# Three more VectorE instructions behind a softmax's reciprocal, and a row maximum kept in bf16

## The chip, the cores and the metric

The program runs on the 8 cores of one Trainium2 chip. Each core works on its own 4096 rows of the activations, and no data passes between cores. The time is that of the slowest core, in microseconds of the device.

## What is computed

One transformer layer: attention over the heads of each token, then a gated feed-forward part, each behind a layer normalisation and with a residual.

```python
def _L0_attn_ref(x, Wq, Wk, Wv, Wfc):
    h, hd = (16, 64)
    Q = (x @ Wq.T).reshape(b, s, h, hd)
    K = (x @ Wk.T).reshape(b, s, h, hd)
    V = (x @ Wv.T).reshape(b, s, h, hd)
    scores = jnp.einsum('bshd,bstd->bsht', Q, K) / math.sqrt(hd)
    attn = jax.nn.softmax(scores, axis=-1)
    out = jnp.einsum('bsht,bstd->bshd', attn, V).reshape(b, s, dm)
    return out @ Wfc.T
x = x + _L0_attn_ref(_layernorm(x, axis=-1), ...)       # x: (4, 8192, 1024)
x = x + _L0_ffn_ref(_layernorm(x, axis=-1), ...)        # 1024 -> 3072 -> 1024, SiLU gate
```

The attention is between the 16 heads of one token: for each of a core's 4096 tokens there is a 16x16 matrix of scores, and its softmax weighs the 16 value vectors of that token. There is no product over the sequence.

## The kernel before

The program has three stages with a barrier between them.

1. Weights (L214 to L307): all weights are transposed by TensorE. The four attention matrices stay in SBUF, the three of the feed-forward part go to HBM.
2. Attention (from L311): 32 tiles of 128 tokens, a token a partition. This stage holds the change.
3. Feed-forward: 8 blocks of 512 tokens, with weights streamed from HBM.

A small scheduler (`Sched`) keeps one list of instructions for each engine. `S.add(engine, fn, waits=..., chain=..., inc=...)` appends to it, so the order of the Python calls is the order on each engine. `chain=True` makes an instruction wait for the one before it on the same engine, by a semaphore; `waits` names other engines' semaphores.

In the attention stage a tile k goes through these steps:

- `load_tile`, `ln1_a`, `ln1_b`, `lnt`, `proj`: the tile `xcT` is loaded, ScalarE takes the sums for the normalisation (L348, L354), VectorE (DVE) makes mean and variance in single columns of `Lr` with two `tensor_scalar`, a product (L369) and a difference (L371), ScalarE takes logarithm and exponential (L374, L378), DVE writes the normalised tile (`xnm`, L382), TensorE transposes it and makes Q, K and V, and ScalarE copies these to `Qs`, `Ks`, `Vs` (L463).
- `front(k)`: the scores, on DVE. For each of four groups g of four heads: the product `gramB` of Q and K (L475, 4096 columns), the add of its two halves (`gh`, L487, 2048 columns) and a sum to 64 scores in `Ss` (L499). Then the maximum over the 16 scores of each head (`Sm`, L508), the subtraction (L516), and the exponential on ScalarE (L523), which leaves `Se`.
- `back_a(k)`: the sum of the exponentials (`Sl`, L532), its reciprocal (`Sr`, L537) and the weights `Aa` (L543) on DVE; then four products `avB` of weights and values on GpSimd (POOL), one for each group (L552). `avB` has two buffers, so groups 2 and 3 wait until TensorE has read groups 0 and 1.
- `back_a2(k)`: TensorE sums `avB` with the identity into `pOT` (L577), ScalarE copies it to `OT` (L593).
- `back_b(k)`: the output projection (L611), and the residual on DVE (`x1p`, L623), whose statistics ScalarE takes.
- `back_b2(k)`: the second normalisation with the same lines L363 to L382 (`xn2m`), eight transposes (L657) and their copies.

The steps of different tiles are interleaved by hand. The slot of tile k is, in the order of the calls: `front(k)`, `back_a(k - 1)`, `back_a2(k - 2)`, `back_b(k - 3)`, `back_b2(k - 4)`, and then, in three of four slots, the normalisation and projections of a tile of the next block (one tile in two of them, two tiles in the third). Behind the last slot follow `back_a(31)` and the rest of the open steps.

The lines that the change touches or surrounds:

```python
323  Sm = e(nc.sbuf_tensor("Sm", [128, 16], F32))
326  Sr = e(nc.sbuf_tensor("Sr", [128, 16], F32))
537  S.add("vector", lambda e: e.reciprocal(Sr[:], Sl[:]), chain=True)
```

Of the kernel before, what the change touches and what calls it, by code (L numbers as in the profile page):

```python
# [7 lines left out]
F32 = mybir.dt.float32  # L8
BF16 = mybir.dt.bfloat16
I32 = mybir.dt.int32  # L10
AF = mybir.ActivationFunctionType
ALU = mybir.AluOpType
# [78 lines left out]
def build_program(taps=(), stop_after=None):  # L91
# [5 lines left out]
    nc = bass.Bass("TRN2", target_bir_lowering=False)  # L97
# [37 lines left out]
    with ExitStack() as TOP:  # L135
# [91 lines left out]
        with ExitStack() as ph:  # L227
            e = ph.enter_context
# [5 lines left out]
            S = Sched(cnt, hwm)  # L234
# [76 lines left out]
        with ExitStack() as ph:  # L311
            e = ph.enter_context
# [7 lines left out]
            Ks = [e(nc.sbuf_tensor(f"Ks{t}", [128, 1024], BF16)) for t in range(4)]  # L320
            Vs = [e(nc.sbuf_tensor(f"Vs{t}", [128, 1024], BF16)) for t in range(8)]
            Ss = e(nc.sbuf_tensor("Ss", [128, 256], F32))
            Sm = e(nc.sbuf_tensor("Sm", [128, 16], F32))
            Se = [e(nc.sbuf_tensor(f"Se{i}", [128, 256], BF16)) for i in range(4)]
            Sl = e(nc.sbuf_tensor("Sl", [128, 16], F32))
            Sr = e(nc.sbuf_tensor("Sr", [128, 16], F32))
            Aa = [e(nc.sbuf_tensor(f"Aa{i}", [128, 256], BF16)) for i in range(4)]
            gramB = [e(nc.sbuf_tensor(f"gramB{i}", [128, 4096], BF16))
                     for i in range(2)]
# [11 lines left out]
            S = Sched(cnt, hwm)  # L341
# [185 lines left out]
            def back_a(k):  # L527
                s, tt = divmod(k, 4)
                e4 = k % 4
                S.add("vector",  # L530
                      lambda e, e4=e4:
                      e.reduce_sum(Sl[:, 0:16].rearrange("p (a b) -> p a b", b=1),  # L532
                                   bass.AP(Se[e4][:].tensor, Se[e4][:].offset,
                                           [[256, 128], [1, 16], [16, 16]]),
                                   AX.X),
                      waits=[("aex", k + 1)])
                S.add("vector", lambda e: e.reciprocal(Sr[:], Sl[:]), chain=True)  # L537
                am_w = []
                if ("pool", k - 4) in cap:
                    am_w.append(("apl", cap["pool", k - 4]))  # L540
                S.add("vector",
                      lambda e, e4=e4:
                      e.tensor_tensor(Aa[e4][:].rearrange("p (t h) -> p t h", h=16),  # L543
                                      Se[e4][:].rearrange("p (t h) -> p t h", h=16),
                                      bass.AP(Sr[:].tensor, Sr[:].offset,
                                              [[16, 128], [0, 16], [1, 16]]),
                                      ALU.mult),
                      waits=am_w, chain=True, inc="amx")
                for g in range(4):
                    S.add("gpsimd",  # L550
                          lambda e, e4=e4, g=g, k=k:
                          e.tensor_tensor(  # L552
                              avB[g % 2][:].rearrange("p (t h d) -> p t h d",
                                                      t=4, d=64),
                              bass.AP(Aa[e4][:].tensor, Aa[e4][:].offset + 64 * g,
                                      [[256, 128], [16, 4], [1, 16], [0, 64]]),
                              bass.AP(Vs[k % 8][:].tensor,
                                      Vs[k % 8][:].offset + 256 * g,
                                      [[1024, 128], [64, 4], [0, 16], [1, 64]]),
                              ALU.mult),  # L560
                          waits=[("amx", k + 1), ("aot", 4 * k + g - 1)],
                          inc="apl")
                cap["pool", k] = S.n("apl")
# [125 lines left out]
            def a1(k):  # L689
                if k >= 0:  # L690
                    back_a(k)
# [83 lines left out]
        with ExitStack() as ph:  # L775
# [17 lines left out]
            S = Sched(cnt, hwm)  # L793
# [129 lines left out]
```

How the kernel before makes its waits and increments, by code:

```python
                    def f(e):  # L71
                        for op in ops:
                            waits = list(op["waits"])
                            for tok in op["deps"]:
                                waits.append(selfcount[tok])
                            for (s, v) in waits:
                                key = (eng_name, s)
                                if v > 0 and hwm.get(key, 0) < v:
                                    e.wait_ge(sems[s], v)
                                    hwm[key] = v
                            ins = op["fn"](e)
                            if op["inc"] is not None:
                                ins.then_inc(sems[op["inc"]], op["incn"])
                            elif op["selfneed"]:
                                ins.then_inc(sems["sf" + eng_name], 1)
# [71 lines left out]
                    def f(e, k=k):  # L157
                        e.nop().then_inc(sems["ph"], 1)
                        e.wait_ge(sems["ph"], NENG * k)
# [7 lines left out]
                @blk.sync  # L167
                def _(sy):
                    t0 = cnt.get("tapd", 0)
                    add = [0]
                    def issue(dst, src):
                        sy.dma_start(dst, src).then_inc(sems["tapd"], 16)
                        add[0] += 16
                    for (_, fn) in todo:
                        fn(issue)
                    sy.wait_ge(sems["tapd"], t0 + add[0])
                    cnt["tapd"] = t0 + add[0]
```

## Time and profile before

| | us |
|---|---|
| three runs | 3925.12, 3932.15, 3969.2 |
| median | 3932.15 |
| the profiled execution | 3932.16 |
| its slowest core's span | 3930.3 |
| spans of all cores | 3898.4 to 3930.3 |

Busy time on the slowest core, in us: TensorE's matmuls 2275.6 (58% of the span), DVE 2040.3 (52%), POOL 1131.8 (29%), ScalarE 685.1 (17%). These shares are averages over three stages with different limits. In the page's 40 slices of the span DVE is at 6 to 9 tenths from slice 7 to slice 26, which is the attention stage, and at 1 tenth behind it, where TensorE goes to 7 to 9. The page says that busy spans on POOL are rough, and that an engine's idle time costs nothing where the engine doesn't set the pace.

### The profile page before, as it was taken

The page shows a single profiled execution, that of the slowest core. Times are in us where ns is not written, and L with a number is a line of the kernel's source. Part 1 is how long each engine was busy: PE and PEld are TensorE (multiplying, and loading weights), DVE is VectorE, ACT ScalarE, POOL GpSimd, SP SyncE. Part 2 cuts the span into 40 slices and gives each one's busy share as a digit, 9 for nine tenths or more (in the row PEclk, how much of TensorE's full clock was granted, in tenths as well). Part 3 has the DMA queues.
Part 4 walks back from the last instruction along what each step waited for, and adds up shares of the span by engine and source line. Part 5 has one row for each costly group of instructions (what it writes and reads, how often), then busy time and mean ns, then how long its engine had stood idle before and what let it go on. Part 6 is the DMA issues. An engine that isn't in the chain of part 4 may idle for free. (4 is left out here: it accounts for less than half of the span.)

```text
span 3930.3 us, 38110 instructions; the slowest of 8 cores (3898.4 to 3930.3 us)
## 1 busy us (share of the span) xinstructions
PE 2275.6 (58%) x12352; PEld 1179.2 (30%) x12352; DVE 2040.3 (52%) x2209; ACT 685.1 (17%) x1691; POOL 1131.8 (29%) x450
## 2 busy tenths in 40 slices
PE   4333354544545345453554453468869788797887
PEld 2111122232323233222232232323324333343333
DVE  5433369786977887869868789411111111111111
ACT  0122231212122212121221211121101111010110
POOL 1000005444444464536344545601101011010110
PEclk9999986766667666667665676689989999999999
DMA  5446300001000001000000000034445444443443
GB/s 94 126 153 203 114 19 1 22 11 33 11 22 22 22 17 27 22 22 22 11 23 21 27 6 11 22 113 140 150 138 159 130 149 142 151 159 126 153 144 140
DMA packets 109629, 302.38 MB, mean 77 GB/s; under 512 B 13184, under 2 KB 29568, under 8 KB 108416
## 3 DMA queue, kind: packets, MB, share of 16 engines
q1 hardware_dynamic: 68736, 159.41, 13.1%
q0 software_dynamic: 32640, 121.65, 10.1%
q10 hardware_dynamic: 8064, 18.88, 1.2%
q8 instruction: 108, 1.77, 0.2%
q14 instruction: 81, 0.66, 0.1%
HBM read 247.46 MB, written 60.82 MB: 78 GB/s over the span
## 5 line engine op out<-in xcount | busy, mean ns | idle before, releaser
L552 POOL TENSOR_TENSOR avB<-Aa,Vs 128x4096 bf16<-128x4096 bf16 x128 | 964.6, 7556 | 1237.9 <-PE pOT L577 761.4
L577 PE MATMUL pOT<-ident,avB 128*128 128x128 bf16 x4096 | 370.4, 275 | 349.5 <-POOL avB L552 349.5
L839 DVE TENSOR_TENSOR hseg<-sg,pU 128x512 bf16<-128x512 bf16 x192 | 132.0, 688 | 710.9 <-PE pU L834 683.7
L577 PEld LDWEIGHTS pOT<-ident,avB 128*128 128x128 bf16 x4096 | 353.0, 127 | 368.2 <-issue 363.2
L820 PE MATMUL pG<-x2s,wgS 128*128 128x512 bf16 x1536 | 376.0, 389 | 125.2 <-DMA wgS<-d_wgT 124.1
L475 DVE TENSOR_TENSOR gramB<-Qs,Ks 128x4096 bf16<-128x4096 bf16 x128 | 420.7, 3286 | 29.0 <-ACT Vs L463 15.4
L834 PE MATMUL pU<-x2s,wuS 128*128 128x512 bf16 x1536 | 370.0, 384 | 19.7 <-DMA wuS<-d_wuT 19.6
L487 DVE TENSOR_TENSOR gh<-gramB 128x2048 bf16<-128x2048 bf16 x128 | 356.0, 2781 | 14.0 <-DVE gramB L475 0.9
L862 PE MATMUL pD<-hseg,wdC 128*128 128x512 bf16 x1536 | 350.2, 385 | 15.9 <-DMA wdC<-d_wdT 14.6
L274 PE MATMUL wps<-ident,wstg_b 128*128 128x128 bf16 x832 | 190.4, 264 | 286.0 <-ACT wstg_b L253 133.4
L657 PE MATMUL pT<-ident,xn2m 128*128 128x128 bf16 x256 | 54.4, 268 | 514.0 <-DVE xn2m L382 479.8
L809 POOL DMA_DIRECT2D wuS<-d_wuT x192 | 103.1, 537 | 805.9 <-PE pU L834 752.8
L499 DVE TENSOR_REDUCE Ss<-gh 128x64 f32<-128x2048 bf16 x128 | 292.6, 2286 | 13.6 <-DVE gh L487 0.5
L879 DVE TENSOR_TENSOR yst<-pT,x1s 128x128 f32<-128x128 f32 x256 | 64.0, 287 | 434.5 <-PE pT L872 434.2
L296 DVE CAST wpk<-wps 128x128 bf16<-128x128 f32 x576 | 142.9, 287 | 209.4 <-PE wps L274 207.8
L820 PEld LDWEIGHTS pG<-x2s,wgS 128*128 128x128 bf16 x1536 | 149.7, 99 | 320.9 <-issue 156.4
L825 ACT ACTIVATE sg<-pG 128x512 bf16<-128x512 f32 x192 | 114.6, 597 | 678.8 <-PE pG L820 678.7
L834 PEld LDWEIGHTS pU<-x2s,wuS 128*128 128x128 bf16 x1536 | 151.4, 99 | 210.9 <-issue 38.1
L862 PEld LDWEIGHTS pD<-hseg,wdC 128*128 128x128 bf16 x1536 | 147.8, 99 | 195.6 <-issue 32.1
L274 PEld LDWEIGHTS wps<-ident,wstg_b 128*128 128x128 bf16 x832 | 86.6, 104 | 389.7 <-issue 362.1
L371 DVE TENSOR_TENSOR Lr<-Lr 128x1 f32<-128x1 f32 x64 | 191.2, 2988 | 7.2 <-DVE Lr L369 0.8
L657 PEld LDWEIGHTS pT<-ident,xn2m 128*128 128x128 bf16 x256 | 25.3, 104 | 553.4 <-issue 547.0
(78 smaller groups left out, 2032.6 us busy)
## 6 DMA issues: line engine op xcount, KB each, us to landing
wuS<-d_wuT POOLq DMA_DIRECT2D x192, 256.0 KB, 3.3
wgS<-d_wgT SPq DMA_DIRECT2D x192, 256.0 KB, 2.6
wdC<-d_wdT POOLq DMA_DIRECT2D x64, 768.0 KB, 4.5
xcT<-x SPq DMA_DIRECT2D x32, 512.0 KB, 5.7
d_x<-x1p SPq DMA_DIRECT2D x32, 512.0 KB, 3.8
x1s<-d_x SPq DMA_DIRECT2D x8, 2048.0 KB, 14.8
y<-yst SPq DMA_DIRECT2D x32, 512.0 KB, 4.3
wstg_i<-wg SPq DMA_DIRECT2D x24, 512.0 KB, 3.9
```

The source lines that it names most:

```text
L274: e.matmul(wps[b % 2][:, 0:128], wstg_b[j % 4][:, b * 128:(b + 1) * 128], ident[:], start=True, stop=True),
L296: e.tensor_copy(pdst(e), wps[b % 2][:, 0:128]),
L371: Sch.add("vector", lambda e: e.tensor_sub(Lrt[:, 5:6], Lrt[:, 3:4], Lrt[:, 4:5]), chain=True, inc="aln")
L475: e.tensor_tensor(gramB[g % 2][:].rearrange("p (t h d) -> p t h d", t=4, d=64), bass.AP(Qs[tt][:].tensor, Qs[tt][:].offset, [[1024, 128], ...
L487: e.tensor_tensor(gh1[:].rearrange("p (a b) -> p a b", b=32), bass.AP(gramB[g % 2][:].tensor, gramB[g % 2][:].offset, [[4096, 128], [64, 6 ...
L499: e.tensor_reduce(Ss[:, 64 * g:64 * (g + 1)] .rearrange("p (a b) -> p a b", b=1), gh1[:].rearrange("p (a b) -> p a b", b=32), AX.X, ALU.add),
L552: e.tensor_tensor(avB[g % 2][:].rearrange("p (t h d) -> p t h d", t=4, d=64), bass.AP(Aa[e4][:].tensor, Aa[e4][:].offset + 64 * g, [[256, ...
L577: e.matmul(pOT[:, 128 * b:128 * (b + 1)], avB[g % 2][:, 1024 * i + 128 * b: 1024 * i + 128 * (b + 1)], ident[:], start=(g == 0 and i == 0 ...
L820: e.matmul(pG[h % 2][:], wgS[h % 2][:, j * 128:(j + 1) * 128], x2buf[xp][j][:], start=(j == 0), stop=(j == 7)),
L834: e.matmul(pU[h % 2][:], wuS[h % 2][:, j * 128:(j + 1) * 128], x2buf[xp][j][:], start=(j == 0), stop=(j == 7)),
L839: lambda e, h=h: e.tensor_mul(hseg[h][:], sg[h % 2][:], pU[h % 2][:]),
L862: e.matmul(pD[c % 2][:], wdC[c % 2][:, k * 128:(k + 1) * 128], hseg[k][:], start=(k == 0), stop=(k == 23)),
```

## The change

The maximum `Sm` is kept in bf16 where it was f32. Behind the reciprocal three instructions are added on DVE, each on 128x16 f32 and each waiting for the one before: `Snr = Sl * Sr`, `Snr = 2 - Snr`, `Sr = Sr * Snr` (one Newton step on the reciprocal). `Aa` follows as before.

```diff
-            Sm = e(nc.sbuf_tensor("Sm", [128, 16], F32))
+            Sm = e(nc.sbuf_tensor("Sm", [128, 16], BF16))
             Se = [e(nc.sbuf_tensor(f"Se{i}", [128, 256], BF16)) for i in range(4)]
             Sl = e(nc.sbuf_tensor("Sl", [128, 16], F32))
             Sr = e(nc.sbuf_tensor("Sr", [128, 16], F32))
+            Snr = e(nc.sbuf_tensor("Snr", [128, 16], F32))
@@
                 S.add("vector", lambda e: e.reciprocal(Sr[:], Sl[:]), chain=True)
+                S.add("vector", lambda e: e.tensor_mul(Snr[:], Sl[:], Sr[:]),
+                      chain=True)
+                S.add("vector",
+                      lambda e: e.tensor_scalar(Snr[:], Snr[:], -1.0, 2.0,
+                                                ALU.mult, ALU.add),
+                      chain=True)
+                S.add("vector", lambda e: e.tensor_mul(Sr[:], Sr[:], Snr[:]),
+                      chain=True)
```

## Rows read from the trace of the kernel before

**Rows 1.** Busy us and instruction count of each engine in the attention stage.

```profile
core 5: us, PE busy (x) PEld busy (x) DVE busy (x) ACT busy (x) POOL busy (x), PEclk, DMA share, GB/s
485.00:2590.00 2105.00, 997.66 (x6656) 619.33 (x6656) 1630.74 (x928) 457.64 (x1377) 964.56 (x128) 0.68 0.07 20
```

**Rows 2.** POOL's waits in that stage: us in total, times, longest.

```profile
POOL avB L552 <- PE pOT L577: 761.4, 32, 45.0
POOL avB L552 <- DVE Aa L543: 476.5, 31, 237.0
```

**Rows 3.** Single lines of DVE: duration ns min/median/max, first and last start.

```profile
L475 DVE TENSOR_TENSOR gramB<-Qs,Ks x128: 2291/2293/8669, 531.3 to 2467.9; 128x4096 bf16<-128x4096 bf16 x128
...
L487 DVE TENSOR_TENSOR gh<-gramB x128: 1224/1226/7867, 533.7 to 2470.3; 128x2048 bf16<-128x2048 bf16 x128
...
L371 DVE TENSOR_TENSOR Lr<-Lr x64: 158/160/6883, 490.2 to 2579.7; 128x1 f32<-128x1 f32 x64
...
L516 DVE TENSOR_TENSOR Se<-Ss,Sm x32: 425/426/3994, 556.4 to 2474.7; 128x256 bf16<-128x256 f32 x32
...
L543 DVE TENSOR_TENSOR Aa<-Se,Sr x32: 425/426/427, 583.5 to 2493.4; 128x256 bf16<-128x256 bf16 x32
...
L363 DVE TENSOR_SCALAR Lr<-Lr,c_ni x64: 213/214/216, 489.3 to 2578.8; 128x1 f32<-128x1 f32 x64
```

**Rows 4.** Time line of DVE, 2470 to 2494: start us, us, instruction, idle before it.

```profile
2475.77 0.25 DVE L537 RECIPROCAL Sr<-Sl 128x16 f32<-128x16 f32 x1
2476.12 0.42 DVE L543 TENSOR_TENSOR Aa<-Se,Sr 128x256 bf16<-128x256 bf16 x1
2476.47 0.68 DVE L623 TENSOR_TENSOR x1p<-pA,xcT 128x512 f32<-128x512 f32 x1
...
2478.49 5.30 DVE L369 TENSOR_TENSOR Lr<-Lr 128x1 f32<-128x1 f32 x1
2483.90 6.88 DVE L371 TENSOR_TENSOR Lr<-Lr 128x1 f32<-128x1 f32 x1
2491.57 0.81 DVE L382 TENSOR_SCALAR xn2m<-x1p,Lr 128x1024 bf16<-128x1024 f32 x1 [0.79 <-ACT Lr L378]
...
2493.36 0.42 DVE L543 TENSOR_TENSOR Aa<-Se,Sr 128x256 bf16<-128x256 bf16 x1
```

**Rows 5.** Time lines of POOL and then of DVE, 2154 to 2229, two places of the second pair.

```profile
2154.44 15.11 POOL L552 TENSOR_TENSOR avB<-Aa,Vs 128x4096 bf16<-128x4096 bf16 x2 [29.17 <-PE pOT L577]
2171.45 14.02 POOL L552 TENSOR_TENSOR avB<-Aa,Vs 128x4096 bf16<-128x4096 bf16 x2 [1.90 <-DVE Aa L543]
2211.62 16.06 POOL L552 TENSOR_TENSOR avB<-Aa,Vs 128x4096 bf16<-128x4096 bf16 x2 [26.16 <-PE pOT L577]
...
2154.80 7.86 DVE L487 TENSOR_TENSOR gh<-gramB 128x2048 bf16<-128x2048 bf16 x1
...
2165.84 3.99 DVE L516 TENSOR_TENSOR Se<-Ss,Sm 128x256 bf16<-128x256 f32 x1
...
2212.75 8.05 DVE L475 TENSOR_TENSOR gramB<-Qs,Ks 128x4096 bf16<-128x4096 bf16 x1
2220.90 7.86 DVE L487 TENSOR_TENSOR gh<-gramB 128x2048 bf16<-128x2048 bf16 x1
```

**Rows 6.** Groups of DVE by line, same shape: busy us, mean ns, idle before, releaser.

```profile
L290 DVE TENSOR_SCALAR WqJ<-wps,c_qk 128x128 bf16<-128x128 f32 x64 | 19.5, 347 | 20.8 <-PE wps L274 20.8
...
L296 DVE CAST WvJ<-wps 128x128 bf16<-128x128 f32 x64 | 15.7, 287 | 11.0 <-PE wps L274 11.0
```

**Rows 7.** Time line of POOL behind the last slot.

```profile
2499.18 27.98 POOL L552 TENSOR_TENSOR avB<-Aa,Vs 128x4096 bf16<-128x4096 bf16 x4 [8.42 <-PE pOT L577]
```

**Rows 8.** Groups of DVE by line: busy us, mean ns, idle before, releaser.

```profile
L371 DVE TENSOR_TENSOR Lr<-Lr 128x1 f32<-128x1 f32 x64 | 191.2, 2988 | 7.2 <-DVE Lr L369 0.8
L516 DVE TENSOR_TENSOR Se<-Ss,Sm 128x256 bf16<-128x256 f32 x32 | 35.0, 1094 | 3.3
```

## The prediction

> **What bounds the kernel now.** I read the page first: the chain that ended last lies almost wholly in the feed-forward stage, so it says nothing about the stage that is edited. The next view is therefore busy time by stage [rows 1]. Attention takes 2105.00 us, with VectorE (DVE) busy for 1630.74 us (77%) at a granted TensorE clock of 0.68; the feed-forward stage is TensorE's and has none of the edited lines. Everything that the edit can do, it does in these 2105 us, that is 65.8 us for each of 32 tiles.
>
> Then who waits for whom [rows 2]. GpSimd (POOL) waits in two places: for `Aa` (L543), 31 times, 476.5 us in all, and for TensorE's `pOT` matmuls, 32 times. So POOL works through a tile's four `avB` products in two pairs: groups 0 and 1 start as soon as DVE has written `Aa`, groups 2 and 3 when TensorE has read group 0. With one exception, which comes below, POOL is idle when `Aa` is being made.
>
> Then how long single instructions take [rows 3]. A `gramB` product takes 2.29 us at its median and up to 8.67, the add `gh` 1.23 and up to 7.87, and a subtraction on one column of `Lr` (L371) 0.16 and up to 6.88. The surplus is 6.4 to 6.7 us at most, and in the time lines [rows 4, 5] it falls where POOL runs an `avB` product, itself 7.0 us (a pair is 14.01): a DVE instruction with two operands in SBUF stands still while POOL holds its product, and the other way round. `Aa`, with the same kind of operands, never does: 425 to 427 ns in all 32.
>
> The time line of DVE around one `Aa` [rows 4] shows what sets the pace. `Aa` starts at 2476.12. POOL begins right behind it. DVE goes on with `x1p` and the statistics, meets the lock at L369 (5.30 us instead of 0.16), meets it again at L371 (6.88), and is through at 2490.78, 14.66 us after the start of `Aa`, which is POOL's pair plus a start of 0.6. ScalarE's two steps, `xn2m` (2491.57), the transposes on TensorE and the `pOT` matmuls follow, and these release POOL's second pair. Hence everything in a tile hangs from the start of `Aa`; a wait of `x1p` for TensorE ahead of L369 is swallowed by the same lock.
>
> **The change part by part.** (a) Three DVE instructions on 128x16 f32 are put between the reciprocal (L537) and `Aa` (L543), each waiting on the one before. The cost is a duration and the gap that a chained successor shows.
>
> Duration of a multiplication: L371 does one column in 0.160 us at its median [rows 3] and L543 does 256 in 0.426, so a column costs (0.426 - 0.160)/255 = 1.04 ns, and 16 columns 0.160 + 15 x 0.00104 = 0.176 us. Duration of the two-operation `tensor_scalar` with written-out numbers: there is no such row. L363, with its factor read from memory, takes 0.214 for one column [rows 3], so 0.230 for 16: the upper bound. Reading a factor costs about 0.347 - 0.287 = 0.060 at equal shape (L290 against the plain copy L296 [rows 6]); less that, 0.170. I take 0.175, nearer to the plain form, because the new one has no factor in memory either; both ends stay for the range.
>
> Gap: L537 starts at 2475.77, lasts 0.25, and `Aa` starts at 2476.12, 0.10 after its end [rows 4]; L369 ends at 2483.79 and L371 starts at 2483.90, 0.11 behind. I take 0.105. Without a wait the next one starts earlier: `x1p` starts at 2476.47, 0.07 before the end of `Aa`. The Trainium skill (VectorE: DVE Perf Modes, The DRAIN you can't avoid) says that a semaphore behind each VectorE instruction costs nothing over one behind the last. By that rule alone the sum would be the three durations, 0.53 us a tile or 16 us; the trace here disagrees with it, since chained and unchained neighbours differ by some 0.18 us in their starts.
>
> Per tile: 3 x 0.105 + 2 x 0.176 + 0.175 = 0.84 us. The upper end with the slower `tensor_scalar` is 0.90. If the gaps didn't count it would be 0.53.
>
> How many tiles are exposed? Each tile whose `Aa` POOL waits for, 31 [rows 2]. The last one isn't: its `Aa` starts at 2493.36, while POOL starts at 2499.18 on four products in a row, the first two of them the second pair of the tile before, because TensorE held it up [rows 7]. That tile's first own product begins some 20 us after its `Aa`, and this covers 0.84 us easily. If that cover were gone, it would cost 0.84 us. Sum: 31 x 0.84 = 26.0 us; the upper end 31 x 0.90 = 27.9.
>
> Nothing cushions it on the other queues. Behind the chained instructions stand `Aa`, `x1p` and the statistics on DVE; POOL waits for `Aa`, ScalarE for the statistics, TensorE for `xn2m` and for POOL. All start later by the same amount, so the distances between POOL's second pair and DVE's `gramB`, `gh` and reduction stay as they are, because all of these come after `Aa`.
>
> (b) `Sm` becomes bf16. The reduction that writes it (L508) still reads 256 f32 columns, the subtraction (L516) still reads `Ss` in f32. L516 unheld takes 0.426 us, as long as L543 [rows 3], so I put this at nothing. If all of L516's columns went twice as fast, it would save 256 x 1.04/2 = 0.13 us a tile, 4 us; that is the other bound. (c) `Snr` is 64 bytes a partition: no time.
>
> Sum: the profiled execution took 3932.16 us (span 3930.3), the median of the three shown is 3932.15, so both bases agree. 3932 + 26 = 3958 us, up by 0.7%. About 1% (39 us) is what a measurement of this kernel can tell from no change.
>
> **The rivals.**
>
> *A new multiplication meets POOL's lock (slower).* The Trainium skill (SBUF — State Buffer, Who interferes with whom) states the rule: a VectorE instruction with two SBUF inputs and a GpSimd instruction that reads SBUF exclude each other for a whole instruction. In this kernel the mechanism is in the rows: L371 waits up to 6.7 us. Both new multiplications are of this kind. If they met the lock in every tile as L371's group does on average, (191.2/64 - 0.16) = 2.8 us each [rows 8], it would be 31 x 5.6 = 175 us and 4133 us in all. It decides for slower from two meetings of 6.7 us on (26 + 13.4 is over 39). For it: six times L516 has been held by 3.57 us just ahead (3.99 against 0.426; (35.0 - 32 x 0.426)/3.57 = 6.0 [rows 5, 8]). Against it: after such a hold POOL has done its fourth product and idles 1.90 us until `Aa` [rows 5], and it gets no new work before `Aa`, behind the new instructions. The trace bears the rule out, but not its case here.
>
> *The second pair changes its place (slower, or less slow).* Its place among DVE's instructions decides what it costs. At 2154.44 POOL asks while `gramB` runs: `gh` loses 6.63 and L516 3.57, 10.2 us together. At 2211.62 it asks 1.13 us ahead of `gramB`: that loses 5.76 and `gh` 6.63, 12.4 us [rows 5]. In the first case 0.36 us more and POOL would have met `gh` already running; earlier by 2 us, the dear case. TensorE's speed between `xnm` and `pOT` sets it, and its clock is between its levels (1.2 and 2.4 GHz) over the stage, 0.68 on average [rows 1]. If the six cheap tiles turned dear: 6 x 2.2 = 13 us, 3971 us; six dear turned cheap: 3945 us. Against both: all of it hangs from `Aa`, as above.
>
> *The delay is hidden.* If half of the tiles had 0.84 us of slack behind `Aa` (TensorE setting the pace by itself), 13 us would be left: 3945 us. For it: `pOT` is POOL's longer wait, 761.4 us [rows 2]. Against it: that wait starts from `xn2m`, so from `Aa`.
>
> **How the numbers follow.** Forecast as reckoned (3952 to 3965): 0.63. Dear places: 0.17, about 3971, some 0.12 of it over the 1% mark. Lock on the new multiplications: 0.05, over 3971. Hidden or cheap places, or a faster L516: 0.15, 3930 to 3950. Slower by over 1%: 0.12 + 0.05 = 0.17. Faster by over 1% needs 65 us less than reckoned, for which no row has a source: 0.02, out of the last case. Within 1%: 0.81. The range takes the hidden case's 3944 and the dear places' 3974.
>
> **What would show it.** Three new groups of 32 on DVE, near 176, 175 and 176 ns with maxima equal to medians (lock: maxima near 6.9 us). From the start of L537 to that of L543: 1.19 us instead of 0.35. L543's 426 and POOL's 31 waits for `Aa` stay. The stage grows by 26 us and the feed-forward stage by nothing. L516's mean stays at 1.09 us if the second pair keeps its place; a fall means dear tiles. Wrong would be: the stage grown by much less with the three groups in full (slack), gaps near zero (the skill's rule), or a `tensor_scalar` far from 0.18 us.

## The result, and the profile after

Against 15 runs of the kernel before (median 3927.41 us) the changed kernel has a median of 3964.59 us over 15 runs. Some runs of both kernels are slower by up to several per cent, with a lower granted clock on the cores of one die or of both; ratios are taken over the other runs alone. That ratio is 1.0089, with a 95% interval of 1.0066 to 1.0113: 26 to 44 us slower, at the middle 35. All ratios below are against the kernel before, measured on the same chip as the run that they belong to.

In the changed kernel's numbering the lines move by one behind L326 and by nine behind the new instructions: `gramB` is L476, `gh` L488, the subtraction L517, the reciprocal L538, the new ones L539, L542 and L545, `Aa` L552, `avB` L561, the statistics L370 and L372, `xn2m` L383.

Groups of VectorE (DVE) by line, after: busy us, mean ns, idle before (they answer to [rows 3, 8]).

```profile
L476 DVE TENSOR_TENSOR gramB<-Qs,Ks 128x4096 bf16<-128x4096 bf16 x128 | 433.7, 3388 | 29.9 <-ACT Vs L464 16.3 <-DVE Ss L500 0.5
...
L372 DVE TENSOR_TENSOR Lr<-Lr 128x1 f32<-128x1 f32 x64 | 218.6, 3415 | 6.7
...
L517 DVE TENSOR_TENSOR Se<-Ss,Sm 128x256 bf16<-128x256 f32 x32 | 34.6, 1082 | 3.7 <-DVE Sm L509 0.5
...
L552 DVE TENSOR_TENSOR Aa<-Se,Sr 128x256 bf16<-128x256 bf16 x32 | 13.6, 425 | 3.5 <-DVE Sr L545 0.3
...
L539 DVE TENSOR_TENSOR Snr<-Sl,Sr 128x16 f32<-128x16 f32 x32 | 5.6, 176 | 3.7 <-DVE Sr L538 0.5
L545 DVE TENSOR_TENSOR Sr<-Sr,Snr 128x16 f32<-128x16 f32 x32 | 5.6, 175 | 3.7 <-DVE Snr L542 0.5
L542 DVE TENSOR_SCALAR Snr<-Snr 128x16 f32<-128x16 f32 x32 | 5.6, 175 | 3.4
```

The three new groups have the durations that were worked out, and `Aa` is as fast as before. What has grown beside them is `gramB`: its group was busy for 420.7 us before and is for 433.7 now, with the same 128 instructions of the same size. The slowest core, whose rows these are, is core 5 before and core 0 after; on core 0 alone `gramB` went from 418.7 to 433.7 us.

The time line of DVE around one `Aa`, after: start us, us, instruction (it answers to [rows 4]).

```profile
2462.41 0.25 DVE L538 RECIPROCAL Sr<-Sl 128x16 f32<-128x16 f32 x1
2462.76 0.17 DVE L539 TENSOR_TENSOR Snr<-Sl,Sr 128x16 f32<-128x16 f32 x1
2463.05 0.17 DVE L542 TENSOR_SCALAR Snr<-Snr 128x16 f32<-128x16 f32 x1
2463.32 0.17 DVE L545 TENSOR_TENSOR Sr<-Sr,Snr 128x16 f32<-128x16 f32 x1
2463.60 0.42 DVE L552 TENSOR_TENSOR Aa<-Se,Sr 128x256 bf16<-128x256 bf16 x1
...
2465.97 5.30 DVE L370 TENSOR_TENSOR Lr<-Lr 128x1 f32<-128x1 f32 x1
2471.38 6.88 DVE L372 TENSOR_TENSOR Lr<-Lr 128x1 f32<-128x1 f32 x1
2479.05 0.81 DVE L383 TENSOR_SCALAR xn2m<-x1p,Lr 128x1024 bf16<-128x1024 f32 x1 [0.79 <-ACT Lr L379]
```

From the reciprocal to `Aa` it is 1.19 us, as against 0.35 [rows 4], and 1.20 at most in 29 of the 32 tiles. `Aa` to the end of L372 is 14.66 us, `Aa` to `xn2m` 15.45 us, as before. So a tile's work behind `Aa` has moved as a block.

On core 0, from the first `xnm` to the last `xn2m`, attention took 2080.3 us before (498.1 to 2578.4) and takes 2123.0 after (498.1 to 2621.1): 42.7 us more; the eight cores lie between 37.7 and 44.5, 41 in the mean. That is 26 for the new instructions and some 15 beyond them. The extra is not spread evenly. Here are the tiles of the two profiled cores, core 5 before and core 0 after. From one `Aa` to the next, tiles whose second pair keeps its place grow by 0.84 us (14, 29 and 31), some by a third of a us more (in tiles 8, 12, 24 and 30 one pause between two DVE instructions is 0.46 us where it is else 0.11; nothing in the trace says why). Call a place of the second pair dear if POOL asks for it ahead of `gramB`, and cheap if it asks while `gramB` runs. Tiles with one projection have swapped dear and cheap places among themselves (four grow by 3.1 to 3.9 us, four shrink by 1.5 to 2.0), which comes out even at 0.9 us each. But four of the nine tiles whose second pair meets no projection on TensorE grow by 3.3 to 3.4 us. One of them, tile 16, goes from 53.81 to 57.20. Here is its DVE time line, then POOL's.

```profile
1583.37 2.29 DVE L500 TENSOR_REDUCE Ss<-gh 128x64 f32<-128x2048 bf16 x1
1585.76 9.10 DVE L476 TENSOR_TENSOR gramB<-Qs,Ks 128x4096 bf16<-128x4096 bf16 x1
1594.96 7.86 DVE L488 TENSOR_TENSOR gh<-gramB 128x2048 bf16<-128x2048 bf16 x1
...
1585.69 16.06 POOL L561 TENSOR_TENSOR avB<-Aa,Vs 128x4096 bf16<-128x4096 bf16 x2 [7.76 <-PE pOT L586]
```

The same tile in the kernel before, DVE and then POOL:

```profile
1563.71 2.29 DVE L475 TENSOR_TENSOR gramB<-Qs,Ks 128x4096 bf16<-128x4096 bf16 x1
1566.11 7.86 DVE L487 TENSOR_TENSOR gh<-gramB 128x2048 bf16<-128x2048 bf16 x1
...
1576.46 6.54 DVE L475 TENSOR_TENSOR gramB<-Qs,Ks 128x4096 bf16<-128x4096 bf16 x1
...
1564.11 16.75 POOL L552 TENSOR_TENSOR avB<-Aa,Vs 128x4096 bf16<-128x4096 bf16 x2 [8.24 <-PE pOT L577]
```

Before, POOL asked for its second pair 0.40 us after `gramB` had started and waited for it. Now it asks 0.07 us ahead of `gramB`, which then stands for 6.8 us; `gh` behind it loses 6.6 us in either case. Before, the next `gramB` (1576.46) lost another 4.2 us; so the place costs 13.4 instead of 10.9. POOL's second pair is asked for 22.88 us behind `Aa` before and 22.41 behind it after. That is TensorE's doing. Busy us and instructions of TensorE, weight loads, DVE, ScalarE and POOL, then the granted clock, in the stretch in which it begins to read the first pair (18.2 to 23.0 us behind `Aa`), before and after:

```profile
1559.43:1564.23 4.80, 4.47 (x41) 4.11 (x41) 4.49 (x4) 3.10 (x8) 0.12 (x1) 0.50 0.00 0
```

```profile
1581.48:1586.28 4.80, 4.46 (x53) 4.12 (x53) 4.49 (x4) 3.09 (x8) 0.59 (x1) 0.65 0.00 0
```

The granted clock was at its lower level (0.50, 1.2 GHz) over the whole stretch before, and after the change the upper one (2.4 GHz) was granted for the last part of it. TensorE read the pair half a microsecond sooner, and so POOL came in ahead of `gramB`. In the three other tiles that grew so, the same stretch had 0.56 to 0.58 before and has 0.64 to 0.67; in the five that stayed cheap it has 0.50 to 0.56 after.

Half a microsecond is the distance between two cores, though. Core 0 had 0.62 in this stretch of tile 16 before the change, and asked 22.51 us behind `Aa`. `gramB` starts 22.48 behind it, so the place was cheap by 0.03 us, and 0.10 us less (22.41) made it dear. All eight cores show the same edge. In the 72 tiles without a projection (nine on each core), every request up to 22.47 us behind `Aa` meets a dear place (56.4 us or more before, 57.1 or more after) and every later one a cheap place (54.1 at most before, 55.3 after). Three of the 72 were dear before, 29 are after.

### The profile page after: what moved, and what is told of

Same layout as the page of the kernel before. It is cut to its first block and busy times, and to the rows that moved or that the text cites. A ratio compares the mean times of both kernels' runs of the same rounds, so it can differ in the third digit from the quotient of the medians.

```text
span 3968.3 us, 38302 instructions; the slowest of 8 cores (3936.1 to 3968.3 us)
## 1 busy us (share of the span) xinstructions
PE 2262.6 (57%) x12352; PEld 1172.7 (30%) x12352; DVE 2086.0 (53%) x2305; ACT 685.4 (17%) x1691; POOL 1134.6 (29%) x450
## 5 line engine op out<-in xcount | busy, mean ns | idle before, releaser
L561 POOL TENSOR_TENSOR avB<-Aa,Vs 128x4096 bf16<-128x4096 bf16 x128 | 967.0, 7576 | 1278.2 <-PE pOT L586 758.3
L476 DVE TENSOR_TENSOR gramB<-Qs,Ks 128x4096 bf16<-128x4096 bf16 x128 | 433.7, 3388 | 29.9 <-ACT Vs L464 16.3
L488 DVE TENSOR_TENSOR gh<-gramB 128x2048 bf16<-128x2048 bf16 x128 | 356.0, 2781 | 14.0 <-DVE gramB L476 0.9
L372 DVE TENSOR_TENSOR Lr<-Lr 128x1 f32<-128x1 f32 x64 | 218.6, 3415 | 6.7
```

The costliest lines, as they stand in the source:

```text
L372: Sch.add("vector", lambda e: e.tensor_sub(Lrt[:, 5:6], Lrt[:, 3:4], Lrt[:, 4:5]), chain=True, inc="aln")
L476: e.tensor_tensor(gramB[g % 2][:].rearrange("p (t h d) -> p t h d", t=4, d=64), bass.AP(Qs[tt][:].tensor, Qs[tt][:].offset, [[1024, 128], ...
L488: e.tensor_tensor(gh1[:].rearrange("p (a b) -> p a b", b=32), bass.AP(gramB[g % 2][:].tensor, gramB[g % 2][:].offset, [[4096, 128], [64, 6 ...
L561: e.tensor_tensor(avB[g % 2][:].rearrange("p (t h d) -> p t h d", t=4, d=64), bass.AP(Aa[e4][:].tensor, Aa[e4][:].offset + 64 * g, [[256, ...
```

## The experiments

**Theory A**: a tile's pace hangs from the start of `Aa`. A chain ahead of it costs its length in 31 tiles; the rest of the loss is where POOL's second pair falls. **Theory B**: the bf16 `Sm` makes the part that the sum lacks. **Theory C**: DVE is the bound, and each microsecond of its work costs one wherever it stands.

**1. The three instructions alone.** `Sm`, which nobody needs any more at this point, takes the place of `Snr`, so that no array is added.

```diff
-Sm = ... BF16
+Sm = ... F32
-e.tensor_mul(Snr[:], Sl[:], Sr[:]) ...
+e.tensor_mul(Sm[:], Sl[:], Sr[:]) ...      # and so in the other two
```

> The three instructions alone; `Sm` stays f32 and also takes the place of `Snr`, since SBUF is full. Theory A (the chain ahead of `Aa` costs 0.84 us in each of 31 tiles, and the rest of the 37 us comes from POOL's second pair falling ahead of `gramB` in some tiles): 26 us plus 0 to 15 us for the places, so 1.007 to 1.010 of before; spacing of the four starts 0.28 us. Theory B (bf16 of `Sm` makes the 11 us that the sum lacks): exactly the 26 us, 1.0066.

Measured: ratio 1.0102, interval 1.0079 to 1.0125. The three groups are at 175 ns, and `gramB` is at 432.6 us, nearly as in the changed kernel.

The cores of this run also differ in TensorE's clock. Over the attention stage cores 4 and 5 were granted 0.668, cores 0 to 3 0.693 to 0.695. On the two slower-clocked cores `gramB` was busy for 387.0 and 380.8 us, and none of their nine tiles without projections was dear; on the other four it was 430.9 to 433.2 us, with three or four dear tiles each. The stage took 2099 and 2097 us on the two, and 2119 to 2122 on the four: with the lower clock it was shorter.

**2. The bf16 maximum alone.**

```diff
-Sm = e(nc.sbuf_tensor("Sm", [128, 16], F32))
+Sm = e(nc.sbuf_tensor("Sm", [128, 16], BF16))
```

> `Sm` in bf16 alone. Theory A: nothing, 0.998 to 1.002, with L508 at 0.58 us and L516 at 0.43 us unheld. Theory B: about 11 us, 1.003. If the subtraction went faster in bf16: 0.30 us instead of 0.43 and up to 4 us less.

Measured: ratio 0.9987, interval 0.9975 to 0.9998; L516 has the mean of before (1094 ns), L508 as well (580), `gramB` 420.8 us. Its middle is 5 us under the kernel before, and no row of the trace has that as a gain. Theory B falls with these two runs: the whole loss comes with the three instructions, none of it with bf16.

**3. The same three behind `Aa`.** They write to `Sm`, which nobody reads, so the Newton step has no effect on the output here.

```diff
                       waits=am_w, chain=True, inc="amx")
+                S.add("vector", lambda e: e.tensor_mul(Sm[:], Sl[:], Sr[:]), chain=True)
+                S.add("vector", lambda e: e.tensor_scalar(Sm[:], Sm[:], -1.0, 2.0, ALU.mult, ALU.add), chain=True)
+                S.add("vector", lambda e: e.tensor_mul(Sm[:], Sr[:], Sm[:]), chain=True)
```

> The same three instructions, chained, on the same operands, but behind `Aa` and with their result going to a tile that nobody reads, so the Newton step itself has no effect. Theory A (a tile's pace hangs from the start of `Aa`, and what stands between `Aa` and L371 is swallowed by POOL's first pair): -5 to +8 us, ratio 0.999 to 1.002, with L371 still ending 14.7 us after the start of `Aa`, and the third new instruction waiting up to 7 us for POOL. Theory C (VectorE is the bound and each microsecond of its work costs one): 26 to 37 us, 1.007 to 1.009.

Measured: ratio 1.0299, interval 1.0268 to 1.0330, some 117 us slower. Neither theory had this. The time line of DVE:

```profile
1508.60 0.43 DVE L543 TENSOR_TENSOR Aa<-Se,Sr 128x256 bf16<-128x256 bf16 x1
1509.14 0.17 DVE L549 TENSOR_TENSOR Sm<-Sl,Sr 128x16 f32<-128x16 f32 x1
1509.42 6.88 DVE L552 TENSOR_SCALAR Sm<-Sm 128x16 f32<-128x16 f32 x1
1516.40 6.88 DVE L555 TENSOR_TENSOR Sm<-Sr,Sm 128x16 f32<-128x16 f32 x1
1523.20 0.68 DVE L631 TENSOR_TENSOR x1p<-pA,xcT 128x512 f32<-128x512 f32 x1
...
1527.60 0.81 DVE L382 TENSOR_SCALAR xn2m<-x1p,Lr 128x1024 bf16<-128x1024 f32 x1 [1.96 <-ACT Lr L378]
```

The first multiplication slips in before POOL starts, the other two wait out one product of the pair each. The lock as such costs nothing more, since L369 and L371 don't meet it any longer. But `x1p` and ScalarE's sums over it, which used to run under the lock, now come after it: `xn2m` starts 19.00 us behind `Aa` instead of 15.45 [rows 4], and 31 x 3.55 = 110 us is the loss. My expectation counted what DVE waits for and forgot what ScalarE does meanwhile. The `tensor_scalar` with 16 f32 columns meets the lock too (its group has a median of 6876 ns), although only one of its operands is a tensor, while the one on a single column (L363, 213 to 216 ns) [rows 3] never does. The Trainium skill (SBUF — State Buffer, Who interferes with whom) has `tensor_scalar` among the instructions that can take GpSimd's port pair where it runs in a two-port mode. This trace agrees with that.

**4. and 5. Work without the lock, behind `Aa` and ahead of it.** Three chained sums of 16 columns, whose results nobody reads; reductions were never held.

```diff
+S.add("vector", lambda e: e.reduce_sum(Sm[:, 0:1], Sl[:, 0:16], AX.X), chain=True)   # and two more
```

> Three chained sums of 16 columns to one (dummies, their results are read by nobody) behind `Aa`. They have one operand, and reductions never stood still for POOL in the traces (L499: 2285 to 2289 ns). The run with the Newton instructions behind `Aa` was 3% slower because two of them waited out POOL's whole first pair (6.9 us each) and `x1p` came after that. Theory A, mended (work between `Aa` and L369 costs nothing as long as it doesn't wait for POOL's lock): ratio 0.998 to 1.003, L371 still ends 14.7 us after the start of `Aa`, L369 is held 0.8 us less. Theory C (each instruction of VectorE costs its time wherever it stands): 31 x 0.8 = 25 us, 1.0065.

> The same three sums between the reciprocal and `Aa`. Theory A and C alike: 31 x 0.8 = 25 us plus 0 to 12 us for the places of POOL's second pair, 1.006 to 1.010. That `Aa` is what sets the pace is shown by this run and the one behind `Aa` together.

Measured: behind `Aa` 1.0002, interval 0.9970 to 1.0035; ahead of it 1.0085, interval 1.0059 to 1.0112. Each sum takes 170 ns and the starts are 0.27 us apart in both. The time line of DVE behind an `Aa` (fourth run, core 4):

```profile
1594.22 0.43 DVE L543 TENSOR_TENSOR Aa<-Se,Sr 128x256 bf16<-128x256 bf16 x1
1594.75 0.17 DVE L549 TENSOR_REDUCE Sm<-Sl 128x1 f32<-128x16 f32 x1
1595.02 0.17 DVE L551 TENSOR_REDUCE Sm<-Sl 128x1 f32<-128x16 f32 x1
1595.29 0.17 DVE L553 TENSOR_REDUCE Sm<-Sl 128x1 f32<-128x16 f32 x1
...
1597.50 4.39 DVE L369 TENSOR_TENSOR Lr<-Lr 128x1 f32<-128x1 f32 x1
1602.00 6.88 DVE L371 TENSOR_TENSOR Lr<-Lr 128x1 f32<-128x1 f32 x1
```

L369 is held for 0.91 us less than in [rows 4], and L371 ends 14.66 us behind the start of `Aa` as it did there. The same 0.8 us cost nothing measurable behind `Aa` and 33 us ahead of it. Theory C falls, and the pace-setting place of `Aa` is shown. `gramB` is at 441.2 us in the second, the dear places again.

**6. Two Newton steps.**

```diff
 S.add(... Snr = Sl * Sr ... Snr = 2 - Snr ... Sr = Sr * Snr)
+S.add(... the same three once more ...)
```

> Two Newton steps instead of one, six chained instructions ahead of `Aa`. Theory A: 31 x 1.68 = 52 us plus -5 to +15 us for places, so 1.012 to 1.017 of before. If the whole 37 us of the change were the price of the three instructions: 74 us, 1.019.

Measured: ratio 1.0168, interval 1.0153 to 1.0183, some 66 us. 52 of them are the chain; `gramB` has grown by 25.5 us in all, and L517, which lost 20.7 - 32 x 0.426 = 7 us to the lock, 14 us less than before. The chain alone, 52 us, lies outside the measured interval (60 to 72 us). Twice the 35 us of the change, 70, lies inside it, so the time alone can't tell a fixed price per step from the chain plus places. In the rows, 52 for the chain, 25.5 more for `gramB` and 14 less for L517 make 63 us.

```profile
L476 DVE TENSOR_TENSOR gramB<-Qs,Ks 128x4096 bf16<-128x4096 bf16 x128 | 446.2, 3486 | 30.2 <-ACT Vs L464 16.5 <-DVE Ss L500 0.5
```

**7. Three instructions that don't wait for each other.** They read only `Sl` and stand for the Newton step, which is left out; `Aa` waits for the reciprocal and for the last of them.

```diff
+                rec = ("vector", len(S.ops["vector"]) - 1)
+                S.add("vector", lambda e: e.tensor_mul(Ss[:, 0:16], Sl[:], Sl[:]))
+                S.add("vector", lambda e: e.tensor_scalar(Ss[:, 16:32], Sl[:], -1.0, 2.0, ALU.mult, ALU.add))
+                S.add("vector", lambda e: e.tensor_mul(Ss[:, 32:48], Sl[:], Sl[:]))
```

> Three instructions of the same kinds and sizes between the reciprocal and `Aa`, but each reading only `Sl` and none waiting for another, so the Newton step is left out; `Aa` waits for the reciprocal and for the last of them. Theory A with gaps as the unchained neighbour shows (start to start 0.08 us less than the duration): 2 x 0.10 and one chained gap, about 0.1 + 0.1 + 0.28 = 0.48 us a tile, 15 us, plus 0 to 12 us for places: 1.004 to 1.007. If a wait costs nothing between neighbours: the same spacing of 0.28 us as in the chained form and the time of the change, 1.009.

Measured: ratio 1.0031, interval 1.0004 to 1.0059.

```profile
1543.11 0.25 DVE L537 RECIPROCAL Sr<-Sl 128x16 f32<-128x16 f32 x1
1543.28 0.11 DVE L539 TENSOR_TENSOR Ss<-Sl 128x16 f32<-128x16 f32 x1
1543.31 0.16 DVE L541 TENSOR_SCALAR Ss<-Sl 128x16 f32<-128x16 f32 x1
1543.38 0.17 DVE L543 TENSOR_TENSOR Ss<-Sl 128x16 f32<-128x16 f32 x1
1543.65 0.42 DVE L549 TENSOR_TENSOR Aa<-Se,Sr 128x256 bf16<-128x256 bf16 x1
```

From the reciprocal to `Aa` it is 0.54 us; so the three cost 0.19 us a tile where the chained three cost 0.84. Most of the price of the change is the waiting of one for the other. The Trainium skill's sentence on semaphores (VectorE: DVE Perf Modes, The DRAIN you can't avoid), by which they come free in a row of `tensor_copy`, does not hold for these instructions. The time's middle, 12 us, lies just under the expected range, and its interval excludes the 1.009 of a wait that costs nothing between neighbours.

**8. and 9. POOL's second pair half a microsecond later.** A memset on POOL (524 ns in the trace), on columns that the product overwrites.

```diff
                 for g in range(4):
+                    if g == 2:
+                        S.add("gpsimd", lambda e: e.memset(avB[0][:, 0:512], 0.0),
+                              waits=[("aot", 4 * k + 1)])
```

> The changed kernel with a POOL memset of 512 bf16 columns (about 0.5 us) ahead of the third `avB` product, so that POOL's second pair asks later. Theory A (in four tiles of the changed kernel the pair asks a few tenths of a us before `gramB` and costs 12 to 13.4 us instead of 10.8; in four others it asks 0.1 to 0.3 us before the last `gramB`): these eight turn cheap, 15 to 20 us less than the changed kernel, ratio to before about 1.004 to 1.006, no `gramB` held by 6.5 us or more in them. If places don't matter: the time of the changed kernel or up to 16 us more (31 x 0.5).

> The kernel before with the same memset. Theory A: its places are mostly cheap already, with margins of 0.1 to 0.46 us on the cheap side, which grow; 5 us less to 5 us more than before, 0.998 to 1.002. If each delay of POOL costs its length: 16 us more, 1.004.

Measured: with the change 1.0066, interval 1.0048 to 1.0083; without it 1.0017, interval 1.0006 to 1.0027. The changed kernel gets some 9 us faster by a delay, if the middles are taken, half of what was expected; the two intervals overlap. The trace shows the mechanism more clearly than the time. In the nine tiles without projections the pair now asks 0.74 to 1.11 us behind the start of `gramB`, and none of them takes more than 55.3 us; the attention stage takes 2094 to 2104 us on the eight cores, against 2116 to 2126 in the changed kernel, 24 less in the mean; the group `gramB` has fallen from 433.7 to 377.5 us:

```profile
L476 DVE TENSOR_TENSOR gramB<-Qs,Ks 128x4096 bf16<-128x4096 bf16 x128 | 377.5, 2949 | 30.0 <-ACT Vs L464 16.3 <-DVE Ss L500 0.5
...
L517 DVE TENSOR_TENSOR Se<-Ss,Sm 128x256 bf16<-128x256 f32 x32 | 63.2, 1974 | 3.7 <-DVE Sm L509 0.5
```

Part of it comes back at L517, 28.6 us. Why the whole time shows less than the stage does is not shown. In one tile (877.96) the first new multiplication stood for 5.93 us: the pair had asked behind `gh`, and POOL's fourth product came after L517. That is the first rival of the prediction, once in 32 on this core:

```profile
L539 DVE TENSOR_TENSOR Snr<-Sl,Sr x32: 174/175/5928, 585.1 to 2507.7; 128x16 f32<-128x16 f32 x32
```

In the kernel before, the same delay moves nothing by 1%, as expected, and makes it at most 11 us slower.

**10. The statistics without the lock.** The variance's product and difference as `tensor_scalar` on single columns, same values.

```diff
-                Sch.add("vector", lambda e: e.tensor_mul(
-                    Lrt[:, 4:5], Lrt[:, 2:3], Lrt[:, 2:3]), chain=True)
-                Sch.add("vector", lambda e: e.tensor_sub(
-                    Lrt[:, 5:6], Lrt[:, 3:4], Lrt[:, 4:5]), chain=True, inc="aln")
+                Sch.add("vector", lambda e: e.tensor_scalar(
+                    Lrt[:, 4:5], Lrt[:, 2:3], Lrt[:, 2:3], None, ALU.mult), chain=True)
+                Sch.add("vector", lambda e: e.tensor_scalar(
+                    Lrt[:, 5:6], Lrt[:, 4:5], -1.0, Lrt[:, 3:4],
+                    ALU.mult, ALU.add), chain=True, inc="aln")
```

> The kernel before with the variance's product and difference (L369, L371) written as `tensor_scalar` with single columns as factors, the same values; only one operand is a tensor, so they should not stand still for POOL. Theory A (POOL and the two-operand instructions of VectorE exclude each other, and the time between is waiting): both at about 0.2 us in all 64, `xn2m` 12 us earlier in each tile, and `gramB` meets the lock in their place; the gain is what ScalarE and TensorE get done meanwhile, part of the 195 us that VectorE waits for `xnm`: 40 to 150 us less, 0.96 to 0.99. If they still meet the lock: no change, 1.00.

Measured: ratio 0.9671, interval 0.9612 to 0.9729, some 129 us faster than the kernel before.

```profile
L369 DVE TENSOR_SCALAR Lr<-Lr x64: 212/214/215, 491.3 to 2438.6; 128x1 f32<-128x1 f32 x64
...
L384 DVE TENSOR_SCALAR xn2m<-x1p,Lr x32: 811/2766/5408, 765.8 to 2439.9; 128x1024 bf16<-128x1024 f32 x32
```

The two instructions that stood still for 328 us together (191.2 + 157.2 - 64 x 2 x 0.16) don't any more. `xn2m` now meets the lock, for 2 us at the median, and `gramB` does so more (496.4 us): the lock's time hasn't gone, but `xn2m`, and with it ScalarE and TensorE, is through 8 us sooner behind `Aa` in most tiles, not the 12 expected.

**11. The change on top of that.** The diff of the change and the one above together.

> The changed kernel with the variance in `tensor_scalar` form. Theory A: the chain ahead of `Aa` costs the same here as in the kernel before, 26 us and up to 15 for places, on top of the 0.967 of that form alone: 0.972 to 0.978. If the Newton step were hidden once the statistics no longer wait: 0.967.

Measured: ratio 0.9719, interval 0.9678 to 0.9761, 0.0048 or 19 us above the form without the change. The interval holds 0.972 to 0.976 of theory A's range. The 0.9671 of no cost lies just below it, but that number has an interval of its own (0.9612 to 0.9729) which overlaps, so the times alone don't settle it. The stage does: from the first `xnm` to the last `xn2m` it takes 1929 to 1944 us on the eight cores in run 10 and 1971 to 1980 here, 34 more in the mean, as theory A has it (26 to 41).

In this kernel the new instructions do meet the lock, in the last tile and on all eight cores. They stand for 5.8, 6.7 and 6.7 us:

```profile
2383.34 5.93 DVE L541 TENSOR_TENSOR Snr<-Sl,Sr 128x16 f32<-128x16 f32 x1
2389.38 6.88 DVE L544 TENSOR_SCALAR Snr<-Snr 128x16 f32<-128x16 f32 x1
2396.37 6.88 DVE L547 TENSOR_TENSOR Sr<-Sr,Snr 128x16 f32<-128x16 f32 x1
```

It costs nothing there: from the `Aa` of the tile before to the last `xn2m` it is 95 us in this run and in run 10, since POOL is still busy with the tile before.

**12. TensorE reads the first pair sooner.** With the statistics as above, `back_a2` is cut in two: the matmuls of groups 0 and 1 are issued at the end of the slot before, ahead of the next transposes and projections.

```diff
+                back_a2(4 * s, 0)          # groups 0 and 1 only
                 if s < 7:
                     load_tile(4 * (s + 1) + 2)
                     ...
                     proj(4 * (s + 1))
```

> The variance in `tensor_scalar` form, and TensorE reads the first two `avB` products of a tile ahead of the next tiles' transposes and projections, not behind them, so that POOL's second pair can start while VectorE waits for ScalarE. Theory A: the second pair asks 15 to 17 us behind the start of `Aa` in all tiles instead of up to 50 us, part of its 14 us then falls into VectorE's waits for `xnm`: 50 to 150 us less than the 0.967 of the first edit alone, 0.93 to 0.955. Rival: TensorE then waits for POOL ahead of the projections and ScalarE's chain comes later; 0.967 or more.

Measured: ratio 0.9393, interval 0.9331 to 0.9455, some 239 us faster than the kernel before. POOL's waits in its attention stage (they answer to [rows 2]):

```profile
POOL avB L556 <- DVE Aa L547: 989.7, 31, 237.6
POOL avB L556 <- PE pOT L585: 7.4, 1, 7.4
```

761.4 us of waiting for `pOT` have gone to 7.4: POOL does a tile's four products in one go (28.4 to 31.5 us in all but the last), partly while DVE waits for ScalarE. It is the fastest of all the kernels here.

## Why the prediction was right, and where it was off

- **The price of the instructions**: 176, 175 and 176 ns forecast, 176, 175 and 175 measured, each at most 177; the step from the reciprocal to `Aa` 1.19 us in both (in 29 of 32 tiles; 1.39 to 1.55 in the other three). A tile whose second pair kept its place grew by the 0.84 us of the sum.
- **31 tiles exposed, nothing cushions it**: right. POOL waits for `Aa` 31 times after as before, and the same 0.8 us cost 33 us ahead of `Aa` and nothing behind it (runs 4 and 5).
- **Distances behind `Aa` stay as they are**: this step failed. It is true of DVE's own 14.66 us, and not of POOL's second pair, whose request depends on the speed of TensorE. The term that stood at 0 for it was worth 15 us on core 0 (`gramB` 418.7 to 433.7) and 15 us over the eight cores (416.4 to 431.6 us of `gramB` in the mean). With 26 that makes 41, the mean growth of the stage. The rival of the dear places had the mechanism and the size (13 us, 3971 us), but the net growth came in other tiles. Of the six with L516 held four did turn dear, and four others turned cheap in their stead. What was left over came from the tiles without projections, where POOL's request stood 0.23 to 0.46 us behind the start of `gramB` on the profiled core, and 0.03 on core 0 (tile 16), a margin that I hadn't put down.
- **"A fall of L516's mean means dear tiles"**: this sign was blind. The mean stayed (1094 and 1082 ns) with six holds before and six after, while eight tiles changed their places.
- **The bf16 maximum at nothing**: right within what can be measured (0.9975 to 0.9998, no row changed).
- **The lock on a new multiplication**: not in the changed kernel; once in 32 on the profiled core when POOL was shifted (run 8), and on all three new instructions of the last tile in run 11. It isn't barred by the order, only by the present places.
- **"A wait of `x1p` is swallowed by the same lock"**: right for DVE and drawn too far afterwards. Run 3 shows that work is hidden under the lock only if it doesn't push `x1p` behind it.
- **The total**: 3958 us is 7 us under the measured median, and its ratio of 1.0066 to the base of that time stands at the lower end of the measured interval. The missing term of the places is the size of that difference or somewhat more. That the time fell into the forecast's own 3952 to 3965 is in part luck: it does so by 0.4 us, and it lies as near to the rival's 3971 as to 3958.

What stays open: why TensorE's upper clock is granted sooner in these tiles. The rows show the clock and what followed from it, on different cores of one run too (run 1), but no run here set it. Nor is it shown why run 2 lies 0.13% under the kernel before.

## What to carry to other kernels

Find the instruction from which the other engines' work hangs, and price added work by whether it stands ahead of it or behind; the busy share of the engine says nothing about that. Chained tiny instructions cost mainly their waits: three that waited for each other took 0.84 us, three that did not 0.19. Where two engines lock each other out, look for small instructions that stand in a long hold (here 0.16 us that took 2.7 on average), write them in a form that isn't locked out, and look how many tenths of a microsecond separate a cheap order from a dear one before calling a shift free.

## What the runs showed of the hardware that I had not expected

- A faster TensorE cost time: at a granted clock of 0.64 to 0.67 instead of 0.50 to 0.58 in a stretch of 4.8 us (core 0 after against core 5 before), POOL asked 0.3 to 0.5 us sooner and the tile took 2.4 to 2.6 us longer beyond the 0.84. In run 1 the stage was 20 to 25 us longer on the cores with 0.693 to 0.695 than on those with 0.668.
- A `tensor_scalar` on 16 f32 columns in SBUF was held by POOL's product for 6.7 us (run 3), one on 1024 f32 columns for up to 5.3 us (run 11, profiled core; 4.7 in run 10), one on a single column never (64 of 64 at 212 to 215 ns, run 10).
- Unchained instructions on 16 columns started 0.03 and 0.07 us apart (run 7), chained ones 0.28.
